# A mixer and mixture-of-experts layer on one core: the D-times-x term by TensorE, the dt projection inside the swiglu, the output projection in halves, four expert sums on VectorE, half of the convolution later

## What is computed

```python
h = embed(tokens) + position                              # 192 wide
u = rmsnorm(layernorm(h)) ; z, xBC, dt = split(u @ in_proj)
dt = softplus(dt + dt_bias) ; xBC = silu(conv4(xBC) + b)  # x 384, B 64, C 64
y = scan(x, B, C, dt)          # 24 heads of 16: h = exp(dt*A)*h + dt*x*B ; y = C.h
y = (y + D * x) * silu(z) ; mix = y @ out_proj
v = rmsnorm(mix) ; h = h + mix + (silu(v @ w_gate) * (v @ w_up)) @ w_down
x2 = layernorm(h)              # routing: best 2 of 4 groups, best 2 experts in them
h = h + shared_expert(x2) + sum_e weight_e * expert_e(x2)
```

## Time and profile before

| | us |
|---|---|
| median of 3 runs (1013.69 to 1015.32) | 1014.93 |
| the profiled execution | 1016.41 |
| its span, first to last instruction | 1014.4 |
| one repetition (start of the third gate product, 460.30 and 518.25) | 57.95 |
| in one stretch of 58.00 us of the loop: PE / DVE / ACT / POOL busy | 50.25 / 40.00 / 35.63 / 21.31 |

### The profile page before, as it was taken

How to read it: one execution, slowest core, us unless ns; L and a number is a source line. 1 busy time by engine, 2 the same in 40 slices (tenths; PEclk the granted TensorE clock), 3 DMA queues, 4 the chain that set the end, 5 groups by cost and what they waited for, 6 DMA issues and landing times.

```text
span 1014.4 us, 22717 instructions
## 1 busy us (share of the span) xinstructions
PE 825.3 (81%) x7120; PEld 637.8 (63%) x7120; DVE 660.8 (65%) x1629; ACT 585.1 (58%) x1307; POOL 345.4 (34%) x508
## 2 busy tenths in 40 slices
PE   3363898888888888888888888888888888888867
PEld 2232676666667666666767666666766666676656
DVE  5565675757667685766768575766768576665524
ACT  3574565665656666665656566565666666565423
POOL 1222333343324344333433334332434433242402
PEclk9675999999999999999999999999999999999988
DMA  8200000000000000000000000000000000000000
GB/s 221 81 1 12 2 6 15 2 20 0 19 0 5 14 0 19 0 19 0 5 14 4 15 0 19 0 20 0 5 14 0 19 0 19 0 5 9 1 8 8
DMA packets 16466, 15.22 MB, mean 15 GB/s; under 512 B 6322, under 2 KB 15224, under 8 KB 16184
## 3 DMA queue, kind: packets, MB, share of 16 engines
q1 hardware_dynamic: 16440, 14.89, 5.5%
HBM read 10.69 MB, written 4.19 MB: 15 GB/s over the span
## 4 chain that ended last, share of the span: by engine, by line
PE 42%; DVE 23%; issue 16%; ACT 13%; POOL 3%; DVEq 1%; ACTq 1%; DMA 0%; POOLq 0%; SPq 0%
PE bank L1305 20%; DVE mr L1024 5%; DVE xa L966 4%; PE bank L1471 4%; PE bank L1513 3%; PE bank L1588 3%; PE bank L1537 3%; DVE w_raw L1188 2%; ACT L687 2%; ACT xk L651 2%; ACT L812 2%; ACT er L706 2%; DVE e_ge L1117 2%; POOL t L476 1%; PE bank L1450 1%
## 5 line engine op out<-in xcount | busy, mean ns | idle before, releaser
L1024 DVE SCALAR_TENSOR_TENSOR mr<-er,gm 128x512 f32<-128x512 f32 x192 | 129.2, 702 | 58.1 <-ACT er L706 57.7
L540 POOL TENSOR_TENSOR w_raw<-w_raw 128x384 f32<-128x384 f32 x96 | 99.2, 1034 | 145.9 <-ACT w_raw L767 143.6
L778 ACT ACTIVATE sg<-bank 128x256 f32<-128x256 f32 x144 | 55.3, 384 | 136.2 <-PE bank L1305 135.9
L1588 PE MATMUL bank<-w2t,w_raw 128*128 128x192 f32 x576 | 116.4, 329 | 7.4 <-ACT w_raw L767 7.4
L706 ACT ACTIVATE er<-bank 128x512 f32<-128x512 f32 x192 | 104.3, 597 | 30.4 <-PE bank L1450 29.9
L1471 PE MATMUL bank<-mr,xd 128*32 128x128 f32 x1536 | 90.9, 288 | 28.0 <-DVE mr L1024 26.6
L966 DVE SCALAR_TENSOR_TENSOR xa<-xr,cw_,xa 128x256 f32<-128x256 f32 x192 | 101.4, 536 | 4.4 <-ACT xa L617 0.4
L1305 PE MATMUL bank<-x_h,w_hi 128*128 128x256 f16 x288 | 79.9, 277 | 29.6 <-DVE w_raw L1188 27.5
L1188 DVE TENSOR_TENSOR w_raw<-sg,bank 128x256 f32<-128x256 f32 x144 | 60.3, 420 | 61.5 <-ACT sg L778 56.3
L1588 PEld LDWEIGHTS bank<-w2t,w_raw 128*128 128x128 f32 x576 | 90.5, 190 | 13.3 <-ACT w_raw L767 9.6
L737 ACT ACTIVATE sg<-bank 128x256 f32<-128x256 f32 x96 | 36.9, 384 | 105.2 <-PE bank L1305 104.8
(11 more groups left out here) (233 smaller groups left out, 2160.4 us busy)
## 6 DMA issues: line engine op xcount, KB each, us to landing
out<-w_raw SPq DMA_DIRECT2D x16, 192.0 KB, 2.0
w_raw<-weights SPq DMA_DIRECT2D x1, 1924.0 KB, 9.6
wt_raw<-weights SPq DMA_DIRECT2D x2, 962.0 KB, 14.9
pos<-position SPq DMA_DIRECT2D x16, 96.0 KB, 2.8
tok<-tokens SPq DMA_DIRECT2D x16, 70.0 KB
sums<-lj SPq DMA_DIRECT2D x16, 64.0 KB, 2.2
ri<-sums SPq DMA_DIRECT2D x64, 12.0 KB
w2t<-w SPq DMA_DIRECT2D x1, 864.0 KB, 19.7
```

Source lines behind the costliest of these rows:

```text
L540: pool.tensor_tensor(acc[:], acc[:], wt_out[:, e % NWT], ALU.add).then_inc(acc_done, 1)
L778: act.activation(sg[:, e % 2, :], p_pair[e % 2][:, 0:NB * Q], ACT.Silu).then_inc(sx_ready, 1)
L1024: ve.scalar_tensor_tensor(mr[:, r % NER], er[:, r % NER], 1.0, gm[:, b, :].unsqueeze(1).to_broadcast([128, HG, Q]), ALU.min, ALU.mult)\
L1588: ins = pe.matmul(p_out[(e + 1) % 2][:, b * D:(b + 1) * D], hh[:, e % NHH, b * Q:(b + 1) * Q], w2t[:, e, :], start=True, stop=True)
```

## The change

1. D*x: ScalarE makes three 128x128 diagonal matrices once at the start (`skip`). In each scan TensorE multiplies them with `xs` into `p_y` ahead of units 0, 2 and 4 (`skipped_x(b, k)`), and the units' products add to that. `xk`, ScalarE's `skipped_x` and GpSimd's addition to `t1` are gone; `scanned` waits for `t1_ready`.
2. `project_out` works on one sequence at a time, and the exponents of units 2 and 3 stand between and behind the halves. ScalarE's `mixed` comes after unit 2 of the exps rather than after unit 1.
3. `project_dt` stands ahead of the last down product of the swiglu and writes to `p_pair[0]`; `steps_dt` stands ahead of `scan(f, 1)`. `norm2_apply` follows unit 4, `turn_x` too. ScalarE loads the silu table right after `split_x`.
4. GpSimd sums the first NP = 5 experts' outputs, VectorE the last ND = 4: the first of these ahead of the last `hh`, the other three behind it.
5. ScalarE's `convolved_in` of the second half (m = 2, 3) and VectorE's taps of m = 1 and m = 2 move into the experts: m = 1 into `route_groups` (where m = 2 was), m = 2 into `route_experts` (where none was).

```diff
             def store(c):
-                sp.wait_ge(out_sum, c * 2 + 2)
+                sp.wait_ge(out_sum, c * ND + ND)
...
-                pool.wait_ge(t1_ready[b], c + 1)
-                pool.wait_ge(xk_ready, c + 1)
-                pool.tensor_tensor(t1[:, b], t1[:, b], xk[:, :, b, :], ALU.add).then_inc(t1_sum[b], 1)
...
+            act.wait_ge(in_first, 48)
+            for k in range(KT):
+                act.activation(skip[:, k], idf[:], ACT.Copy, scale=dsk[:, k:k + 1]).then_inc(setup_a, 1)
...
-            def skipped_x(c):
-                act.wait_ge(xs_ready, c + 1)
-                if later(c):
-                    act.wait_ge(t1_sum[1], c)
-                for k in range(KT):
-                    ins = act.activation(xk[:, k], xs[:, k], ACT.Copy, scale=dsk[:, k:k + 1])
-                ins.then_inc(xk_ready, 1)
...
                     if e == 0:
                         route(c)
-                    for out_ in {2: (0,), 8: (5, 6)}.get(e, (e - 3,) if e > 3 else ()):
+                        if p is not None:
+                            convolved_in(p, 1)
+                    for out_ in {2: (0,), 8: ()}.get(e, (e - 3,) if e > 3 else ()):
                         weigh(c, out_)
...
-                    scan(f, 0, {} if b is None else {2: lambda: mixed(b), 4: lambda: mixed_norm(b)})
+                    scan(f, 0, {} if b is None else {3: lambda: mixed(b), 4: lambda: mixed_norm(b)})
...
                     split_x(b)
+                    act.activation(warm[:], mhalf[:, 0:1], ACT.Silu)
                 if p is not None:
-                    convolved_in(p)
+                    convolved_in(p, 0)
...
             def experts(c, p):
                 for e in range(NX):
+                    if e == NX - 1:
+                        weighed_sum(c, NP)
                     ve.wait_ge(sx_ready, c * NX + e + 1)
...
-                for e in range(NP, NX):
+                for e in range(NP + 1, NX):
                     weighed_sum(c, e)
...
+                if b is not None and p is not None:
+                    steps_dt(p)
                 if f is not None:
-                    scan(f, 1, {} if b is None else {1: lambda: norm2(b), 3: lambda: norm2_apply(b),
-                                                     4: lambda: None if p is None else steps_dt(p)})
+                    scan(f, 1, {} if b is None else {1: lambda: norm2(b), 4: lambda: norm2_apply(b)})
...
+                    skipped_x(b, first // 2)
...
+            def skipped_x(b, k):
+                pe.matmul(p_y[:, k * Q:(k + 1) * Q], skip[:, k], xs[:, k, b, :], start=True, stop=False,
+                          skip_group_check=True)
...
                 down(NF - 2)
+                if p is not None:
+                    project_dt(p, c)
                 down(NF - 1)
...
                     if e >= 2:
 
-                        pe.wait_ge(weighed, c * NP + e - 1)
+                        if e - 2 < NP:
+                            pe.wait_ge(weighed, c * NP + e - 1)
+                        else:
+                            pe.wait_ge(out_sum, c * ND + e - 1 - NP)
...
                 if b is not None:
-                    project_out(b)
+                    project_out(b, 0)
+                if f is not None:
+                    exponents(f, 2)
+                if b is not None:
+                    project_out(b, 1)
+                if f is not None:
+                    exponents(f, 3)
```

More of the change, by code:

```diff
@@ L46 @@
 HG = 4
-DT_AT = 64
 NQ = NH // HG
@@ L133, in program @@
         dsk = sb("dsk", [128, KT])
+        skip = sb("skip", [128, KT, 128])
         spread16 = sb("spread16", [128, KT, 2, 128], F16)
@@ L292, in program @@
         t1_ready = [sem(f"t1_ready{b}") for b in range(NB)]
-        t1_sum = [sem(f"t1_sum{b}") for b in range(NB)]
         sn_done = [sem(f"sn_done{b}") for b in range(NB)]
@@ L309, in program @@
         NX = NE + 1
-        NP = NX - 2
+        NP = NX - 4
+        ND = NX - NP
         h13_done, sx_ready, hh_ready, ex_done, acc_done = (sem(n) for n in (
@@ L641, in convolved_rest @@
                     act.wait_ge(yi_done[1], c)
[L642 removed]
+                    act.wait_ge(yq_done, c * NR)
                 act.activation(xs[:, 2:NM], xa[:, 2:NM], ACT.Silu).then_inc(xs_ready, 1)
                 act.activation(bc[NS:128], xa[0:NS, KT], ACT.Silu).then_inc(b_ready, 1)
[L646 to L652 removed]
             def softplus(c):
@@ L1153, in route_experts @@
             def route_experts(c, p):
-                ranks(c, sv[:], NE, before8, e_gt, e_ge, None, None)
+                ranks(c, sv[:], NE, before8, e_gt, e_ge, p, 2)
             def route_weights(c):
@@ L1270, in body @@
                 if p is not None:
-                    for m in range(2):
-                        for k in range(1, KC):
-                            convolve_tap(p, m, k)
+                    for k in range(1, KC):
+                        convolve_tap(p, 0, k)
                 if b is not None:
@@ L1279, in body @@
                         setup_rest(1)
-                    for m in range(2, NM):
+                    for m in range(1, NM):
                         for k in range(1, KC):
@@ L1459, in scan @@
                     pe.wait_ge(y_sum[0], c + 1)
+                if b == 0 and not later(c):
+                    pe.wait_ge(setup_a, 1 + KT)
                 for first in range(0, NQ, 2):
                     for q in (first, first + 1):
-                        if b * NQ + q + 2 < NR:
+                        if 3 < b * NQ + q + 2 < NR:
                             exponents(c, b * NQ + q + 2)
+                    skipped_x(b, first // 2)
                     for q in (first, first + 1):
@@ L1500, in state_share, with project_out @@
                 pe.matmul(p_misc[:, 0:DI], bt[:, b, :], xw[:, b, :], start=True, stop=True).then_inc(sn_done[b], 1)
-            def project_out(c):
-                if not later(c):
-                    pe.wait_ge(in_late, 96)
-                    pe.wait_ge(dx_ready, 2)
-                pe.wait_ge(y_ready[0], c + 1)
-                pe.wait_ge(y_ready[1], c + 1)
-                if later(c):
-                    pe.wait_ge(out_sum, c * 2 - 1)
-                for b in range(NB):
-                    for k in range(DI // 128):
-                        ins = pe.matmul(p_out[0][:, b * D:(b + 1) * D], y[:, b, k, :], wo[:, k, :],
-                                        start=(k == 0), stop=(k == DI // 128 - 1))
-                ins.then_inc(m_out, 1)
+            def project_out(c, b):
+                if b == 0:
+                    if not later(c):
+                        pe.wait_ge(in_late, 96)
+                    if later(c):
+                        pe.wait_ge(out_sum, c * ND - 1)
+                pe.wait_ge(y_ready[b], c + 1)
+                for k in range(DI // 128):
+                    ins = pe.matmul(p_out[0][:, b * D:(b + 1) * D], y[:, b, k, :], wo[:, k, :],
+                                    start=(k == 0), stop=(k == DI // 128 - 1))
+                if b == NB - 1:
+                    ins.then_inc(m_out, 1)
             def turn_v(c):
@@ L1631, in body @@
                     pre_turn(p)
-                def tokens_steps_and_turn():
-                    if p is not None:
-                        project_dt(p, b)
-                    turn_x(b)
                 if f is not None:
-                    scan(f, 1, {} if b is None else {3: tokens_steps_and_turn}, p)
+                    scan(f, 1, {} if b is None else {4: lambda: turn_x(b)}, p)
                 elif b is not None:
```

60 lines of the change are left out of this document (28 added, 32 removed).

## The result

| | before | after |
|---|---|---|
| median, us | 1015.12 (1013.69 to 1015.45, 4 runs) | 963.69 (962.24 to 964.78, 4 runs) |
| span of the profiled execution, us | 1014.4 | 962.2 |
| granted clock, mean of the span | 0.962 | 0.966 |
| one repetition (first exponents to first exponents) | 57.95 | 54.60 |

The ratio is 0.9495, with a 95% interval of 0.9479 to 0.9512: 51.4 us less. The forecast was 958.0 with a range of 944 to 982, so the forecast was 5.7 us too low and the range holds the time.

The account below looks back on a forecast made before the run. No engine was taken as full; chains passing between engines set the time. 14 repetitions × −4.0 us and −1.5 for the ends gave −57.5 from 1016.4, forecast 958 us, with an 8-in-10 range of 944 to 982.

Parts of the forecast that it names:

- (a): Exponents and output projection, up to the first gate product: earlier third exponents, less skip products; −0.4 us per repetition.
- (b): Swiglu's second wait, at the third gate product: the whole wait goes without the xk work; −0.8 us per repetition.
- (c): Third gate product to pre_turn: a new wait, as h_next follows the second gt; +0.5 us per repetition.
- (d): Second scan, to project_in_x: steps_dt leaves VectorE's units and unit 4 fills the wait before xn; −1.05 us per repetition.
- (e): First expert steps, to step 6: three taps move from the front into the ranking's gaps; −1.05 us per repetition.
- (f): Experts' end, to the next exponents: ScalarE goes from last silu to table load without weightings; −1.2 us per repetition.
- R1: Rival: VectorE stays the bound in the experts, moved taps taking full length and meeting additions twice; about 975 us, chance 0.15.
- the rule: VectorE with two SBUF inputs and GpSimd block each other for whole instructions, so taps moved into the ranking would suffer.
- R2: Rival at the experts' end: GpSimd's fifth addition or VectorE's first sum is 1.2 us late; 975 us, chance 0.09.
- R3: Rival: slower, a late fifth addition delaying the last hh, down products and next exponents; 1028 us at 5 us lateness, chance 0.04.
- R4: Rival: nothing, all gains given back where TensorE waits next; 1013 to 1017 us, chance 0.02.
- The ends: Program's start and end: second call of body +1.4 us, last two calls −1.2 and −1.7; together −1.5.

Follow-up runs that it names:

- experiment 1: Changed kernel with the skip term D*x back on ScalarE and GpSimd, without diagonal matrices and TensorE's skip products: 967.31 us.
- experiment 3: Changed kernel with GpSimd adding seven experts' outputs and VectorE summing two, none ahead of the last hh: 982.17 us.
- Experiment 4: Changed kernel with both halves of convolved_in and all six taps ahead of the experts again, none in the expert ranking: 973.4 us.
- experiment 5: Changed kernel with the dt projection back in the second scan, norm2_apply after unit 3 and the silu table loaded in the experts: 980.97 us.
- experiment 8: Changed kernel with the embedding's pre_norm after the first gate product instead of the second: 957.43 us.
- experiment 6: Changed kernel with the first sequence's state read ahead of units 0 and 1 in the first scan: 949.03 us.
- experiment 2: Changed kernel with the output projection in one piece again, ahead of the exponents of units 2 and 3: 963.85 us.
- experiment 10: Changed kernel with the first sequence's state read ahead of units 0 and 1 and the output projection whole: 960.14 us.
- experiment 12: Changed kernel with GpSimd's five expert additions covering 8 columns of each sequence instead of 192, other sums left out: 943.49 us.
- experiment 11: Kernel before the change with only the first sequence's state read moved ahead of units 0 and 1: 1014.03 us against 1013.98 beside it.

## Why the prediction came out as it did

In the prediction's own steps, measured as distances between the same instructions of a repetition in both traces:

| step | forecast | measured | from |
|---|---|---|---|
| (a) first exponents to first gate product | −0.4 | +0.20 | 9.56 to 9.76 |
| (b) to third gate product | −0.8 | −0.81 | 3.50 to 2.69 |
| (c) to `pre_turn` | +0.5 | +0.46 | 4.59 to 5.05 |
| (d) to `project_in_x` (second scan) | −1.05 | −1.00 | +0.06, then 8.72 to 7.66 |
| (e) to expert step 6 | −1.05 | −0.96 | 17.23 to 16.27 |
| (f) to the next first exponents | −1.2 | −1.25 | 10.28 to 9.03 |
| sum | −4.0 | −3.35 | |

**(b) to (f)** are right within 0.1 us each, and their causes stand in the rows after: no wait at the third gate product, the new one of 0.31 before `pre_turn` (0.5 by starts), `dx` at 503.13 inside the table load of 501.99, the fourth unit directly ahead of `xn`, the table load right behind the last silu. Experiments 1, 3, 4, 5 and 8 put a price on each, per repetition: 0.3 for (b) with (c), 1.2 for (f), 0.8 for the order of the taps, 1.2 for (d) with ScalarE's tables, 0.5 for the wait of (c).

**(a) is the step that failed.** The prediction said that "units 2 and 3 gain" from the earlier third exponents. Unit 2 does, but VectorE takes `t1` before unit 3, and `t1` waits for the state read. TensorE does that read behind the whole projection, four exponents, the skip product and units 0 and 1, which is the same work in either order of the halves. So the read moved only by what was added: from 3.62 to 3.82 us after the first exponents. `t1`, which unit 2 had held before, now starts 4.79 after them rather than 4.75. The other 0.15 of the +0.20 is unit 3's product behind it, 1.01 us long and 0.86 before:

```profile
510.41 0.86 DVE L1024 SCALAR_TENSOR_TENSOR mr<-er,gm 128x512 f32<-128x512 f32 x1
```

It stands beside GpSimd's decay of the state, 0.84 us long and begun at 509.88 before and at 486.54 after, so they overlap for 0.31 and 0.46 us. The product took 0.68 where it came first (experiment 6) and 1.23 where they overlap for 0.68 (experiment 1). No run has this decay moved by itself, so its share rests on these lengths. The skip product itself was mis-sized: from a row of six for three products I took 0.16 each, but that row counts two passes for a product, and the product takes 0.31 (484.58 to 484.89). About 0.1 of it fell into a wait that had been there before. The square of experiments 2, 6 and 10 shows the mechanism: `t1` needs both, unit 2 early (by the halves) and the read early (by its place). From the corner with neither the one alone is worth 0.2 us, the other alone 3.7, and both 14.8.

**(e), R1 and the rule.** The forecast let one loss stay in the ranking and one in the last taps, and so it was: `e_ge` gave its loss to the tap. Experiment 4 moves it back, and experiment 12 takes both away and prices them at 1.4 us a repetition. The rule weighed in the prediction (the Trainium skill, SBUF — State Buffer, "two separate sides") describes this: the trace agrees in that a tap or a comparison with two SBUF inputs is long beside GpSimd's addition and at its own length when the addition is short. It did not make R1 true, since both meetings were in the kernel before as well; the moved taps only filled gaps. R2 is visible in its beginnings: the first sum waits 0.49 us for the fifth addition, and the first exponents come without a wait right behind the last down products. R3 and R4 did not happen. R1's own sign did not show either: the fifth `hh` comes 23.47 us after the first exp of the second scan, 25.48 before, so 2.0 earlier. (The terms that R1 names, +0.7 or +1.05 in (e) and +0.2 in (c), give −3.1 to −2.75 per repetition and not −3.0 to −2.6, which changes little.)

**The ends.** The second call of `body` forecast +1.4 and showed +1.8 (the first exponents of the first repetition at 98.61 rather than 96.80). ScalarE waits for the taps behind the splitting of weights:

```profile
80.53 0.63 ACT L630 ACTIVATE xs<-xa 128x512 f32<-128x512 f32 x1 [3.87 <-DVE xa L956]
```

The last two calls forecast −2.9 and showed −3.1 (101.36 to 98.25). The 14 repetitions went from 816.24 to 765.34, that is −50.9, of which 14 × −3.35 is −46.9. The other 4 us are irregular repetitions. The first one, counted from first exponents, took 60.38 before and 55.53 after (96.80 to 157.18 and 98.61 to 154.14). Counted from GpSimd's first addition of experts, the kernel before has 57.94 to 57.98 where it is regular, 58.20 once early in the loop, and 59.33 and 58.67 late in the loop. These two, 2.1 us above the others together, are those in whose second scan the granted clock fell. This window view of before shows the first of the falls, to 0.50 in one window, that is to 1.2 GHz from 2.4:

```profile
822.00:824.00 2.00, 1.22 (x22) 0.83 (x22) 1.89 (x4) 0.00 (x0) 0.84 (x2) 1.00 0.00 0
824.00:826.00 2.00, 1.37 (x19) 0.59 (x20) 1.37 (x4) 1.72 (x4) 0.55 (x1) 0.72 0.00 0
826.00:828.00 2.00, 2.00 (x11) 1.44 (x10) 1.14 (x3) 0.78 (x4) 0.45 (x1) 0.50 0.00 0
828.00:830.00 2.00, 2.00 (x23) 1.45 (x22) 0.36 (x2) 1.97 (x4) 1.53 (x3) 0.93 0.00 0
```

The second shows 0.72, 0.50 and 0.92 from 882 to 888 us. Waits alone do not explain when it falls: ahead of the first fall TensorE was busy for 1.22 of 2.00 us, but it was so in the same stretch one repetition earlier (764 to 766 us), and there the clock stayed at 1.00. The trace of experiment 11, the other kernel with the old order, has the same pair of repetitions (59.31 and 58.65) with the same two falls, earlier in the loop. In windows of 15 us the changed kernel shows no clock below 1.00 between 115 and 910 us. The traces of its eleven edits show none between 150 and 850 us either. So the change may have kept the clock up as well, by its fewer waits or otherwise; that was not tried apart.

The repetition's terms overshot by 14 × 0.65 = 9.1 us, and 4.0 came back from repetitions that the forecast had taken as all alike: 958.9 + 9.1 − 4.0 + 0.2 for the ends is 964.2, against 964.0 for the profiled execution. That the forecast is only 5.7 us off the median is in part luck, since these 4.0 us, about which it said nothing, hid almost half of what step (a) and the smaller terms missed.

## What to carry to other kernels

Before counting an earlier start as a gain, walk the consumer's queue one instruction further: here `t1`, between the two units that were to gain, waited for something that the edit left where it was. A step held by two things at once shows nothing when one of them is moved, so try the pair (0.2 and 3.7 us alone, 14.8 together). And a wait moved off one instruction may land on its neighbour: look for what runs on the other engine at that moment, not for the instruction that is long.

## What was not expected of the hardware

- VectorE and GpSimd both pay when they meet. GpSimd's addition of 1.00 us took 1.48 and 1.26 beside taps; the 16-column addition took 0.69 and 0.48 beside them and 0.22 alone, while the taps beside it kept their length. With the short additions it is GpSimd that is held. With the long ones it was VectorE alone where GpSimd had started first (0.99 beside `e_ge` of 1.09), and both where a tap had started just before the addition (520.58 and 520.64).
- A float32 product of 128x128 is shown as two matmuls, 0.22 to 0.31 us from start to start of what follows. A group's count must be halved before dividing.
- The granted clock fell to 1.2 GHz for some 3.5 us twice in the middle of a loop that is otherwise at 1.00, and those repetitions took 1.4 and 0.7 us longer than their neighbours (59.33 and 58.67 against 57.96). Both traces of the old order show it, and none of the twelve of the changed order.
